# Moving four vector instructions inside the inversion of a gated delta rule kernel

## The reference

```
x = L0_attn_x
xn = _layernorm(x)
x = x + attn(xn) + ffn(xn)

# attn, per head and time step, with a state S of 128 x 64:
q, k, v = short_conv(xn @ Wq), short_conv(xn @ Wk), short_conv(xn @ Wv)   # 4 taps, silu; q, k l2-normed
beta = sigmoid(xn @ Wb);  g = -exp(A_log) * softplus(xn @ Wa + dt_bias)
S = S * exp(g_t)
u = (v_t - k_t S) * beta_t
S = S + k_t u^T
o_t = q_t S
out = (rmsnorm(o) * norm_w * silu(xn @ Wg)) @ Wo
```

## Time and profile before

| | us |
|---|---|
| median of three executions | 2689.53 |
| lowest, highest | 2685.06, 2694.64 |
| the profiled execution, its own time | 2694.64 |
| its span from first to last instruction | 2692.9 |

### The profile page before, as it was taken

How to read it: one execution, slowest core, us unless ns; L and a number is a source line. 1 busy time by engine, 2 the same in 40 slices (tenths; PEclk the granted TensorE clock), 3 DMA queues, 4 the chain that set the end, 5 groups by cost and what they waited for, 6 DMA issues and landing times. The chain is left out here.

```text
span 2692.9 us, 93819 instructions
## 1 busy us (share of the span) xinstructions
PE 2284.7 (85%) x36541; PEld 1667.2 (62%) x36542; DVE 1893.5 (70%) x3913; ACT 1355.9 (50%) x3667; POOL 1136.2 (42%) x1143
## 2 busy tenths in 40 slices
PE   4643999999967989889898988989888888988887
PEld 4542999999944646656465565646556564655646
DVE  5663233222238888888889889888888978888785
ACT  0001444444345556665556566565665655566563
POOL 3773444444432615244262534526243342624323
PEclk9997999999988999999999999999999999999999
DMA  5673222222211010000101000010100001010000
GB/s 167 198 258 126 73 72 70 75 72 72 70 38 35 9 37 22 24 21 25 43 7 39 22 24 24 22 43 20 26 22 24 26 20 43 19 28 22 24 25 18
DMA packets 105645, 135.05 MB, mean 50 GB/s; under 512 B 39361, under 2 KB 78817, under 8 KB 105057
## 3 DMA queue, kind: packets, MB, share of 16 engines
q0 software_dynamic: 23552, 61.38, 7.4%
q1 hardware_dynamic: 62448, 40.55, 6.0%
q10 hardware_dynamic: 19312, 28.33, 3.0%
HBM read 76.18 MB, written 54.00 MB: 48 GB/s over the span
## 5 line engine op out<-in xcount | busy, mean ns | idle before, releaser
L1450 DVE SCALAR_TENSOR_TENSOR att_cv<-att_psA,att_cw,att_cv 128x508 f32<-128x508 f32 (+2 forms) x660 | 479.1, 737 | 7.6
L991 PE MATMUL att_psA<-att_xt,att_wqkv 128*128 128x512 f32 x880 | 434.4, 627 | 28.6 <-DMA att_xt<-xn_cols 24.2
L1781 POOL TENSOR_TENSOR att_Sd<-att_S,att_mst 128x1024 f32<-128x1024 f32 x128 | 242.8, 1902 | 363.6 <-DVE att_S L1564 340.4
L991 PEld LDWEIGHTS att_psA<-att_xt,att_wqkv 128*128 128x128 f32 x880 | 159.1, 196 | 194.2 <-issue 161.5
L1768 POOL TENSOR_TENSOR att_qg<-tri_q,att_mst 128x512 f32<-128x512 f32 x32 | 33.4, 1044 | 581.0 <-DMA att_mst<-token_stats 573.2
L734 PE MATMUL moe_psHT<-moe_xT,moe_w1s 128*128 128x128 f32 x2176 | 268.7, 277 | 0.0
L1114 PE MATMUL att_psS<-att_W,att_ktok 128*128 128x128 f32 x2048 | 256.9, 279 | 11.9 <-DVE att_S L1564 6.5
L1114 PEld LDWEIGHTS att_psS<-att_W,att_ktok 128*128 128x128 f32 x2048 | 240.8, 192 | 32.5 <-issue 17.6
L744 PE MATMUL moe_psY<-moe_w,moe_hT 128*128 x1088 | 257.8, 380 | 0.0
L734 PEld LDWEIGHTS moe_psHT<-moe_xT,moe_w1s 128*128 128x128 f32 x2176 | 257.1, 194 | 0.2
L675 ACT ACTIVATE moe_hT<-moe_psHT,moe_b1T 128x128 f32<-128x128 f32 x544 | 155.1, 368 | 202.3 <-PE moe_psHT L734 202.3
(11 more groups left out here) (247 smaller groups left out, 4394.4 us busy)
## 6 DMA issues: line engine op xcount, KB each, us to landing
expert_out<-moe_y POOLq DMA_DIRECT2D x136, 128.0 KB, 2.0
route_x_in<-in_L_attn_x_dram SPq DMA_DIRECT2D x64, 128.0 KB
xn_rows<-route_xn ACTq DMA_DIRECT2D x16, 512.0 KB, 3.6
xn_cols<-route_xnT ACTq DMA_DIRECT2D x16, 512.0 KB, 3.8
moe_w<-in_L_ffn_W_dram ACTq DMA_DIRECT2D x2, 4096.0 KB, 24.2
att_xt<-xn_cols SPq DMA_DIRECT2D x16, 512.0 KB, 4.7
att_xr<-in_L_attn_x_dram SPq DMA_DIRECT2D x64, 128.0 KB, 4.4
out_dram<-att_xr SPq DMA_DIRECT2D x256, 32.0 KB
```

The lines of the kernel that those rows point to most:

```text
L991: last = MM(pair_bank(m, j)[:, h, :], wqkv[:, c, (2 * j + h) * P:(2 * j + h + 1) * P], xt[:, c, :], start=(c == 0), stop=(c == DC - 1))
L1450: last = V.scalar_tensor_tensor(out=late, in0=by_lane(pair_bank(m, j)[:, h, :])[:, :, 0:LT - d], scalar=cw[:, 2 * j + h, TAPS - 1 - d:TAPS ...
L1781: G.tensor_tensor(new, old, bc(mst[:, par, c, 4 + 2 * two:6 + 2 * two, :], 3, DV), op=ALU.mult).then_inc(s["sd_done" if two else "sd_half" ...
```

## The change

In `others` the 18 empty items are gone, and `out(m, 0)` and `out(m, 1)` now come ahead of `read(f, 0)` and `residual(f, 0)`.

```diff
-        ALONE = 18
@@ after_keys, others
                     yield from taps(f, par, 8)
                     yield from taps(f, par, 9)
-                    for _ in range(ALONE):
+                    if m is not None:
+                        out(m, 0)
+                        yield
+                        out(m, 1)
                         yield
                     read(f, par, 0)
                     yield
                     residual(f, 0)
                     yield
-                    if m is not None:
-                        out(m, 0)
-                        yield
-                        out(m, 1)
-                        yield
 
                 invert(f, par, others())
```

## The result

| | median us | runs |
|---|---|---|
| before | 2691.17 | 5 (2685.06 to 2694.64) |
| changed | 2707.68 | 5 (2698.22 to 2717.16) |

The changed kernel is slower by 0.61% (ratio 1.0061, 95% interval 1.0032 to 1.0092). Beside before on two other chips it was slower by more: 1.0098 (1.0076 to 1.0120) and 1.0085 (1.0057 to 1.0113). Forecast were 2697 us and 7 us of loss; the loss is 16 to 23 us. The profiled execution, not one of the five, took 2716.68 us, with a span of 2714.9; it is slower than the median by 9.0 us.

What follows compares the result with a forecast made beforehand. Neither PE (85%) nor DVE (70%) was full; PE was late in every pass, leaving 75.08 us reserve. Terms 7.0 - 3 + 1 + 1.8 = 6.8 us on median 2689.53 gave 2696.3, taken as 2697 for smaller reserve; range 2687 to 2707.

Steps and rivals of the forecast that it cites:

- The delay of 4.0 and 3.4 us: DVE's inversion ends 4.0 us later per pass, 3.4 in five passes where `read` had not started on arrival.
- The reserve: Windows from inversion's end to `solve`, 75.08 us over 16 passes before; forecast to sum to 20 to 25 after.
- The second rival: `solve` waiting for `elim` in most passes, slower than forecast: 2701 to 2706 us, chance 0.17.
- term 1: At `solve`, four passes with too little reserve for the later inversion: 7.0 us lost.
- Term 2: On SP, stores off the way of the next columns' load, which starts earlier: 3 us gained, bounds 0 and 8.
- term 3: PE's stops, read as instruction fetch, lengthened in two passes by the earlier load: 1 us lost, from 0 to 2.5.
- Term 4: PE's clock falling to half after longer idling ahead of `solve`: one case, 1.8 us lost, bounds 0 and 7.2.

Runs made afterwards that it cites:

- e12: Changed kernel with POOL's product into att_qg held back until the inversion has ended: 2702.34 us, ratio 1.0058 to before.
- e6: Changed kernel run again without any edit, on another chip: 2707.04 us against 2683.71 for before, ratio 1.0098.
- e11: Changed kernel run a third time without any edit: 2711.64 us against 2688.37 for before, ratio 1.0085.
- e3: Changed kernel with POOL's product into att_qg held back until the inversion has ended, on a slower chip: 2827.28 us, ratio 1.0063 to before.
- before again: Kernel before run again without any edit, for a second profile: 2684.66 us against 2683.71, ratio 1.0003.
- e8: Kernel before with the stores of chunks 0 and 1 issued by POOL instead of SP, so the load starts early: 2685.35 us, ratio 1.0001.
- e9: Kernel before, with SP's load of the next columns waiting for PE's product of queries and keys: 2680.01 us, ratio 0.9967.
- e10: Changed kernel, with SP's load of the next columns waiting for PE's product of queries and keys: 2692.39 us, ratio 1.0016 to before.
- e13: Changed kernel with half of PE's next projection moved ahead of `solve` in five passes: 2714.39 us, ratio 1.0094 to before.

## Why the prediction was wrong

**What held.** The row-by-row picture: DVE idle before the first sum until L1148, `read` unmoved, ten links behind `residual`. The delay of 4.0 and 3.4 us: without POOL's product the inversions end 15.5 to 15.6 us behind the data in all but the first pass (e12), against 11.5 and 12.1 in before. The reserve: 19.4, 15.8 (e6) and 19.8 us (e11), forecast 20 to 25. That the loss appears as PE waiting for the inverse in the passes with little reserve. The second rival named the place rightly, and its condition came true in part (six to nine passes wait instead of four); its upper end, 2706 us, lay 2 below the measured 2707.7.

**The step that failed is term 1,** 7.0 us of PE waiting for the inverse. The three profiles of the changed kernel have 17.8, 20.9 (e6) and 17.5 us (e11). Over the two profiles of before and these three, the way from `read`'s data to `solve` grows from 259.7 to 275.1 us: 15.4 more, where terms 1 to 3 gave 5. Two things were missing. First, I moved DVE's inversion later and did not ask what it would come to lie beside: POOL's product at the landing of the statistics, 0.75 us in eight passes. With it taken away PE waits 12.1 (e3) and 12.7 us (e12), 5 to 9 less. Second, I took the reserve of one execution, the slowest of three, as given. The same sum over the reserves of before again, with the same 4.0 and 3.4 us, gives 12.8 us from seven passes, which is what e3 and e12 show; for this I had allowed 0.7.

**Term 2 and term 3 cancel.** The earlier load came as forecast (0.1 us behind the gate), but with before's order no gain shows (e8). It lengthens the stops of just the two passes that I had named: over the same profiles the fourth and the fourteenth go from 4.7 to 8.3 us together, 3.6 more, where I had taken 1 and bounded it by 2.5. All stops at that line grow by less, from 29.3 to 31.6 us. The larger miss is that I did not ask whether before's own load comes too early: sent later it is worth 8 us to before and 19 to the changed kernel (e9, e10).

**Term 4** was taken for one pass, 1.8 us; in each profile three waits before the last pass were followed by half clock, about 2 us each. The scans take 6.9 us more (904.7 to 911.6 on average over those profiles). The fall of the clock behind the long waits is in the rows; its cause is not settled by an experiment, since e13 failed to separate it. That e12 shortened the three waits and kept the full clock there speaks for it.

**Two smaller readings** were off without changing the sum. The first pass has 3.16 us of reserve, less than the 3.32 of the pass at 2041.52 and not more. And the section of the Trainium skill's page "VectorE: DVE Perf Modes" that I quoted, "The DRAIN you can't avoid", goes on to say that a next instruction that is not held starts earlier. That fits the independent link of the earlier trace rows, so the trace does not contradict the section as a whole.

The version that beats both kernels is before with the late load (e9), 8.4 us at the median, 0.33%.

## What to carry to other kernels

Leaving places of a filling empty can be right: twelve dependent links fitted the wait for another engine's data, and an instruction whose data are late stops everything behind it. Cover in a profile is not a credit: read it from more than one execution and per pass, and look at what the delayed work will newly lie beside. A transfer whose landing is waited for can still be issued too early: here PE's stops at its own instructions grew with the load beside them.

## What the runs showed of the hardware

A POOL product of two operands (128x512, 1.04 us) stretched the short DVE links beside it: the link under it took 0.9 to 1.1 us instead of 0.2 to 0.25, eight times in each profile of the changed kernel and never with the product held back (e3, e12). Beside the long DVE product behind the last link (1.23 us) it was POOL's that grew, to as much as 1.74 us, and DVE's did not; beside the transpose behind it neither grew by more than about 0.1 us. PE's stops among matmuls that wait for nothing come at steps of 256 of its instructions. With the 512 KB load sent 2 us behind the gate those at `read_queries` were 2.4 us at most in five kernels; with the load sent 0.1 to 0.7 us behind it on average the longest was 3.9 to 5.7.
